# A two-block transformer kernel on one core: batches 1 to 3 of the first projection move into the first attention, and stacks are loaded in chunks of 512 tokens

## The reference, cut to what matters

```python
# block 0 attention, per batch and head
scores = alpha * tanh(q @ k.T / beta)
scores = scores + lam * (tanh(x @ hex_w.T) @ tanh(x @ hex_w.T).T / 2)
scores = scores + 2 * sig * (hexc @ Mh[h] @ hexc.T) / 6        # hexc = tanh(x @ q6_w.T)
out = softmax(causal(scores)) @ v
# block 1 attention
q, k = rope(x @ Wq.T), rope(x @ Wk.T)
out = softmax(causal(q @ k.T / 4)) @ v
```

## Time and profile before

| stage | us from the span's start | length, us |
|---|---|---|
| setup | 0 to 33.8 | 33.8 |
| projection 0, first to last matmul | 39.9 to 289.5 | 249.6 |
| from there to the first score matmul | 289.5 to 342.85 | 53.4 |
| attention 0 | 342.85 to 2521.3 | 2178 |
| rest of block 0, projection 1 | 2521.3 to 3040.7 | 519 |
| loads before attention 1 | 3040.7 to 3069.5 | 29 |
| attention 1 | 3069.5 to 4235.5 | 1166 |
| rest of block 1 | 4235.5 to 4547.3 | 312 |

### The profile page before, as it was taken

One profiled execution on the slowest core, in us unless ns is written; L12 is line 12 of the kernel. 1 busy time (PEld: TensorE's weight loads), 2 busy tenths in 40 slices (PEclk: granted clock), 3 DMA queues, 4 the chain that ended last, 5 costly groups with the idle time before them and its releaser, 6 DMA issues. The chain is left out here.

```text
span 4547.3 us, 67109 instructions
## 1 busy us (share of the span) xinstructions
PE 3916.2 (86%) x23290; PEld 1495.0 (33%) x23298; DVE 2646.7 (58%) x4835; ACT 3480.4 (77%) x3199; POOL 454.1 (10%) x407
## 2 busy tenths in 40 slices
PE   6958888888888888888888767649999999999787
PEld 3422222222222222222222554323333233333466
DVE  5537777777777777777777787851111110111488
ACT  2429999999999999999999213329999999999433
POOL 3530000000000000000000125640000000000133
PEclk9979999999999999999999988879999999999999
DMA  5872222012222112222202445652122221212232
GB/s 166 253 220 52 55 56 55 22 37 56 55 56 55 34 25 56 56 55 55 49 17 48 139 129 161 195 170 78 47 82 61 67 81 47 84 48 82 90 97 83
DMA packets 270543, 372.13 MB, mean 82 GB/s; under 512 B 27499, under 2 KB 214667, under 8 KB 265529
## 3 DMA queue, kind: packets, MB, share of 16 engines
q1 hardware_dynamic: 270244, 368.27, 29.6%
HBM read 238.14 MB, written 130.02 MB: 81 GB/s over the span
## 5 line engine op out<-in xcount | busy, mean ns | idle before, releaser
L861 DVE SCALAR_TENSOR_TENSOR att_prob<-att_tanh,alpha,ps 128x512 f32<-128x512 f32 (+3 forms) x2584 | 1583.5, 661 | 523.7 <-ACT att_tanh L795 352.1
L722 PE MATMUL ps<-att_q,att_k 96*128 96x512 bf16 (+7 forms) x5172 | 1233.3, 352 | 189.9 <-DMA att_v<-v_ones 101.7
L749 PE MATMUL ps<-att_prob,att_v 128*32 128x512 f32 (+3 forms) x10304 | 1213.0, 543 | 11.0 <-ACT att_prob L807 6.2
L795 ACT ACTIVATE att_tanh<-ps,rbeta 128x2048 f32<-128x2048 f32 (+3 forms) x646 | 1111.4, 1720 | 122.7 <-PE ps L722 122.7
L802 ACT ACTIVATE att_prob<-ps 128x1024 f32<-128x1024 f32 (+3 forms) x1290 | 1068.2, 906 | 124.6 <-PE ps L724 114.2
L807 ACT ACTIVATE att_prob<-att_prob 128x2048 f32<-128x2048 f32 (+3 forms) x645 | 1072.0, 1662 | 51.0 <-DVE att_prob L861 48.7
L733 PE MATMUL ps<-att_f,att_g 75*128 75x512 bf16 (+3 forms) x2584 | 855.0, 358 | 182.8 <-DVE att_prob L861 157.1
L722 PEld LDWEIGHTS ps<-att_q,att_k 96*128 96x128 bf16 (+1 forms) x5172 | 424.1, 98 | 1053.4 <-ACT att_prob L802 430.8
L831 DVE STREAM_TRANSPOSE att_ot<-ps 128x512 f32<-128x512 f32 x128 | 91.3, 713 | 1047.4 <-PE ps L749 1010.1
L733 PEld LDWEIGHTS ps<-att_f,att_g 75*128 75x128 bf16 x2584 | 236.6, 97 | 1066.7 <-DVE att_prob L861 1037.8
L749 PEld LDWEIGHTS ps<-att_prob,att_v 128*32 128x32 f32 x10304 | 203.1, 108 | 370.7 <-issue 142.5
(11 more groups left out here) (132 smaller groups left out, 2620.1 us busy)
## 6 DMA issues: line engine op xcount, KB each, us to landing
att_v<-v_ones SPq DMA_DIRECT2D x34, 1024.0 KB
v_ones<-proj_vs SPq DMA_DIRECT2D x128, 256.0 KB, 3.5
att_q<-q_parts SPq DMA_DIRECT2D x102, 256.0 KB
att_k<-k_parts SPq DMA_DIRECT2D x102, 256.0 KB
att_q<-q_parts SPq DMA_DIRECT2D x204, 128.0 KB
att_k<-k_parts SPq DMA_DIRECT2D x204, 128.0 KB
q_parts<-proj_parts SPq DMA_DIRECT2D x64, 384.0 KB, 3.4
k_parts<-proj_parts SPq DMA_DIRECT2D x64, 384.0 KB, 3.0
```

Source lines behind the costliest of these rows:

```text
L722: mm = pe.matmul(out, st[u]["k"][:, h, kb * P:(kb + 1) * P], st[u]["q"][:, h, g * TG + off:(g + 1) * TG], start=True, stop=not mask)
L749: mm = pe.matmul(ps[VW * h:VW * (h + 1), O0 + g % 2, off:TG], st[u]["v"][:, kb, h * VW:(h + 1) * VW], prob[:, k % R, h, off:TG], start=kb ...
L795: th.done(act.activation(tanh_s[:, k % 2, :, off:TG], ps[:, QK0:QK0 + HQ, off:TG], ACT.Tanh, scale=kn["rbeta"][:, 0:1]))
L861: sc.done(dve.scalar_tensor_tensor(prob[:, k % R, h, off:TG], tanh_s[:, k % 2, h, off:TG], kn["alpha"][:, 0:1], ps[:, E0 + h % 2, off:TG], ...
```

## The change

1. `project_phase` of layer 0 handles batch 0 only (`NB=1`). It reads x already transposed (`x0_t`, prepared on the host), so the transposes on TensorE and their copies on ScalarE are gone for layer 0.
2. Batches 1 to 3 of that projection are 108 units inside attention 0: 12 groups of 512 tokens with nine units each (g, q, q, k, k, f, f, v, v). A unit starts at the end of steps 2, 6, 10, ... of each batch, 36 in its 160 steps. TensorE does the unit's matmuls into bank 7, ScalarE takes tanh of g, VectorE copies the others out (in the next step, between heads 1 and 2), GpSimd splits q, k, f and g by itself, and SyncE stores them.
3. Bank 7 is taken from the output: in layer 0 the output has one bank (`OU = 1`), and the first weigh of a query group waits for the transpose of the group before.
4. Parts of `normalise` are taken ahead of head 0 instead of between heads 1 and 2.
5. Stacks are loaded by chunk of 512 tokens into rings (3 of q and f, 6 of k, g and v), 26 DMAs a chunk in layer 0 and 14 in layer 1. The rows in DRAM are ordered so that each partition reads one run. g is stored once instead of once per quad; projection 1 stores each q and k tile by quad, in four DMAs.
6. In layer 1 the mask matmuls are gone. VectorE takes the minimum with a table (`keep`) after exp, two instructions per diagonal step, and weigh(k) waits for it. weigh lags by two steps instead of one.
7. The steps past the last set are gone in both layers.

```diff
-    LAG = 2 if layer == 0 else 1
+    LAG = 2
+    QU, KU = 3, 6
+    QK0, E0, O0, BG = 0, 4, 6, 7
+    OU = 1 if layer == 0 else 2
+    EVERY = 4
+    def unit_at(S):
+        b, s = divmod(S, NHQ * NST)
+        u, rest = divmod(s - 2, EVERY)
+        return b * (GB * NU) + u if b < B - 1 and rest == 0 and 0 <= u < GB * NU and N_UNIT else None
...
+            def project(j):
+                X, kind, m, tile, n = unit(j)
...
+                bg_ev.wait(pe, j - 1)
+                if kind == "f":
+                    mm = pe.matmul(ps[0:n, BG], kn["Cq"][:].rearrange("p q e h -> p (q e h)")[:, m * n:(m + 1) * n], f12[:, X % 2], start=True, stop=True)
+                elif kind == "v":
+                    for t in range(2):
+                        at_t = slice((2 * m + t) * P, (2 * m + t + 1) * P)
+                        for c in range(DC):
+                            mm = pe.matmul(ps[:, BG, t * D:(t + 1) * D], xt_s[:, X % 2, c, at_t], wv_s[:, c, :], start=c == 0, stop=c == DC - 1)
+                else:
+                    for c in range(DC):
+                        lhs = w12_s[:, c, :] if kind == "g" else (wq_s if kind == "q" else wk_s)[:, c, m * P:(m + 1) * P]
+                        mm = pe.matmul(ps[0:n, BG], lhs, xt_s[:, X % 2, c], start=c == 0, stop=c == DC - 1)
+                bg_ps.done(mm)
...
             def weigh(S):
...
+                elif diag:
+                    kept.wait(pe, (it * ND + kb) * 2 + 1)
...
                 if kb == 0:
-                    o_tr.wait(pe, set_of(i, k) * GB + g - 2)
+                    o_tr.wait(pe, n - OU)
...
+            for S in range(N + LAG):
...
+                if layer == 0 and S < N:
+                    extra(S, 2)
+                    extra(S, 3)
+                if unit_at(S) is not None:
+                    project(unit_at(S))
...
+            def evict(j):
+                X, kind, m, tile, n = unit(j)
+                if kind == "v":
+                    bg_ps.wait(dve, j)
+                    v_out.wait(dve, m, X - 1)
+                    bg_ev.done(dve.tensor_copy(vs[:, m, :, :, 0:HD], ps[:, BG].rearrange("p (t h d) -> p t h d", t=2, h=H)))
+                elif kind != "g":
+                    bg_ps.wait(dve, j)
+                    low.wait(dve, tile - 2)
+                    bg_ev.done(dve.tensor_copy(raw[0:n, tile % 2], ps[0:n, BG]))
...
+            def diagonal(S):
+                it, g, kb, off, *_ = at(S)
+                for pair in range(2):
+                    pr.wait(dve, S * 2 + pair)
+                    block = prob[:, S % R, 2 * pair:2 * pair + 2, off:off + P]
+                    kept.done(dve.tensor_tensor(block, block, kn["keep"][:].unsqueeze(1).to_broadcast([P, 2, P]), ALU.min))
...
                 for h in range(HQ):
-                    if h == 2:
-                        normalise(i, due, 2 if g <= 1 else 1)
+                    if h == 0:
+                        normalise(due, 2 if g <= 1 else 1)
+                    if h == 2 and S > 0 and unit_at(S - 1) is not None:
+                        evict(unit_at(S - 1))
...
+            for n in range(QU):
+                load(n)
+                if layer == 0 and n == 0:
+                    for name, t in (("wq", wq_s), ("wk", wk_s), ("wv", wv_s), ("w12", w12_s)):
+                        sp.dma_start(t[:], w[name]).then_inc(w_in, 16)
+                    load_x(0)
+                    load_x(1)
+            LATE = LAG + 3
+            for S in range(LATE, N + LATE):
+                it, g, *_, last = at(S - LATE)
+                n = it * GB + g
+                if last:
+                    if n + QU < NG:
+                        o_tr.wait(sp, n)
...
+                        load(n + QU)
+                    store_o(n)
+                if unit_at(S - LATE) is not None:
+                    store_unit(unit_at(S - LATE))
```

More of the change, by code:

```diff
@@ L42 @@
 MASKED = -1.0e30
+KEEP = 3.0e38
 BOUND = 60.0
@@ new lines, in weigh @@
+            def weigh(S):
+                it, g, kb, off, diag, last = at(S)
+                n, c = it * GB + g, it * GB + kb // CB
+                if layer == 0:
+                    pr.wait(pe, S)
+                elif diag:
+                    kept.wait(pe, (it * ND + kb) * 2 + 1)
+                else:
+                    pr.wait(pe, S * 2 + 1)
+                if kb == 0:
+                    o_tr.wait(pe, n - OU)
+                for h in range(HQ):
+                    mm = pe.matmul(ps[VW * h:VW * (h + 1), O0 + n % OU, off:TG], v_s[:, c % KU, kb % CB, h * VW:(h + 1) * VW], prob[:, S % R, h, off:TG], start=kb == 0, stop=last)
+                pv.done(mm)
@@ L809, in _, with feature @@
-            for k in range(W):
-                step(0, k)
-            for i in range(B * NHQ // U):
-                for k in range(W, NB + W):
-                    step(i, k)
+            def feature(j):
+                X, kind, m, tile, n = unit(j)
+                if kind == "g":
+                    bg_ps.wait(act, j)
+                    if X >= 2:
+                        low.wait(act, tile - 2 * NTL)
+                    bg_ev.done(act.activation(f12[:, X % 2], ps[0:NF, BG], ACT.Tanh))
@@ L866, in _ @@
-            for i in range(B * NHQ // U):
-                due = []
-                for k in range(W, NB + W):
-                    step(i, k, due)
-                assert not due
-def row_max_phase(nc, kn, layer):
+            due = []
+            for S in range(N + LAG + 1):
+                if S > LAG and at(S - LAG - 1)[-1]:
+                    due += [(S - LAG - 1, part) for part in range(4)]
+                if S < N and layer == 0:
+                    sums(S, due)
+                else:
+                    if S < N and at(S)[4]:
+                        diagonal(S)
+                    normalise(due, len(due))
@@ new lines, in _ @@
+            assert not due
+        if layer == 0:
+            @block.gpsimd
+            def _(pool):
+                for c in (hi, rest, mid, low):
+                    c.start(pool)
+                for j in range(N_UNIT):
+                    X, kind, m, tile, n = unit(j)
+                    if kind == "v":
+                        continue
+                    u = tile % 2
+                    src = f12[:, X % 2] if kind == "g" else raw[0:n, u]
+                    bg_ev.wait(pool, j)
+                    parts_out.wait(pool, u, tile // 2 - 1)
+                    hi.done(pool.tensor_copy(parts[0:n, u, 0], src))
+                    hi.wait(pool, tile)
+                    low.wait(pool, tile - 1)
+                    rest.done(pool.tensor_tensor(rem[0:n], src, parts[0:n, u, 0], ALU.subtract))
+                    rest.wait(pool, tile)
+                    mid.done(pool.tensor_copy(parts[0:n, u, 1], rem[0:n]))
+                    mid.wait(pool, tile)
+                    low.done(pool.tensor_tensor(parts[0:n, u, 2], rem[0:n], parts[0:n, u, 1], ALU.subtract))
```

554 lines of the change are left out of this document (325 added, 229 removed).

## The result

The kernel after takes 4608.8 us (median of 4, 4602.7 to 4614.3), the kernel before 4552.4 in the same runs: ratio 1.0122, 95% interval 1.0100 to 1.0144. It is slower by 1.2%. The forecast was 4460, with a range of 4370 to 4575.

What follows compares the result with a forecast made beforehand. TensorE was taken to bound projection 0 and attention 1, ScalarE attention 0. From 4549.15 us, -194 + 187 - 2 - 11 - 11 - 58 - 2 + 1.5 = -89.5 gave 4460 us, range 4370 to 4575.

Steps and rivals of the forecast that it cites:

- (b): Attention 0, third step of a query group: weigh waits for transpose; 0.8 us without unit, 2.5 with q, k, v, 1.55 f.
- Projection 0 and the start: Start to first score matmul: 205.8 us less, mostly from projection 0 handling one batch without transposes (-194).
- The wait for chunk 1: Start of attention 0: chunk 1 lands at 43.8, group 0 is over at 33.5, so 10 us of wait.
- (a): Attention 0, unit in the middle of full steps: exp late by 1.15 us for q, k, v, 0.6 g, 0.25 f.
- (c): Attention 0, unit in step r2 (steps 10, 22, 38), slack only 0.1: 1.6 us more, f 0.7.
- (d): Attention 0, step 2, r2 and third step at once: 2.4 us with a unit, 0.3 without.
- Between the attentions: From attention 0's last output transpose to attention 1's first matmul: 25 us less.
- Attention 1: First matmul to last output transpose: 54 us less; masks off TensorE save 58 over 64 groups, bounds 20 and 80.
- The slower rival: Attention 0: unit and boundary delays add up in full, 353 us in place of 187, total 4626 us; chance 0.15 or 0.13.
- its mark: Sign deciding for the slower rival: idle time of ScalarE in attention 0 over 390 us, from 118.
- Units hide: Rival: TensorE's 280 free us in attention 0 take the units, only the boundaries' 43 remain; 4316 us; chance 0.08.

Runs made afterwards that it cites:

- Run 3: The kernel after, units and one output bank kept, with the transpose of a finished output issued one step earlier in attention 0; 4418.8 us, ratio 0.971.
- run 2: The kernel after without units (first projection does all four batches ahead of attention 0), still with one output bank; 4572.6 us, ratio 1.004.
- Run 5: The kernel after plus seven unread matmuls in front of the weigh that waits for the transpose; 4511.2 us, ratio 0.992 to the kernel before.
- run 9: As run 10, with each piece of a unit issued ahead of its step's third extra matmul, where TensorE waits; 4288.5 us, ratio 0.943.
- run 7: The kernel after with q, k and g units cut into four pieces and the transpose one step earlier; 4386.0 us, ratio 0.964.
- run 10: As run 7, with VectorE's transpose and its copy of a unit moved ahead of the step's first sum; 4338.9 us, ratio 0.954.
- run 8: As Run 3, with whole units two steps later; meant for a group's last step, but none landed there; 4452.1 us, ratio 0.978.

## Why the prediction was wrong

**The step that failed** is (b), the boundary with one output bank, priced at 0.8 us without a unit and 2.5 with one. It let TensorE be idle 1.8 us, then work on at full clock, and put the clock at nothing in the sum. The idle time was right (1.65 at 651.90); the clock behind it was not, and the price of the wait at full clock was too low as well. Attention 0 took 2485 us, over the 2440 that the forecast had named as a sign that it is wrong. Against the 133.1 us of a set with nothing of this, a set with units has 25.3 more. A line through its 11 sets has 0.30 us for each us of half clock; with 23.9 us of it in the mean that is 7.2 for the clock. Run 3 shows 13.2 for the units without the boundary's wait, 1.6 of them for its own 5.5 us of half clock, so 11.6. The other 6.5 are the waits (4.6 in run 2, without units). The forecast had, in the mean over slots filled and empty, 12.0 for the units, 2.7 for the waits and 0 for the clock; in the sets without units it had 2.7, and 8.0 was measured, 4.4 of them clock (16.2 us of half clock at run 2's 0.27) and 3.6 waits. So a set with units cost 10.6 us more than forecast: 7.2 for the clock, 3.8 for the waits, less 0.4 for the units. Over 12 and 4 sets that is 148 us; the shorter undisturbed set (133.1 for 134.8) gives 27 back, and 121 are left, against the 120 to be explained. The split rests on fitted lines and is rough. Run 5 is the kernel after with most of its clock back: 4511 us, inside the forecast's own range of 4400 to 4530.

Point by point:

- **Projection 0 and the start:** -202.3 for -205.8. Its last matmul ends at 101.3 us (98 forecast), its bound is TensorE, right. The wait for chunk 1 was 4 us of TensorE's and 5.4 of ScalarE's, not 10, as the first group's matmuls ran at the lower level of the clock (four scores 1.87 us, for 1.04 in the earlier trace rows) and took up more of the time:

```profile
140.55 1.87 PE L819 MATMUL ps<-att_q,att_k 96*128 96x512 bf16 x4 [39.23 <-DMA att_v<-v_ones]
160.86 1.89 PE L819 MATMUL ps<-att_q,att_k 96*128 96x512 bf16 x4 [4.04 <-DMA att_v<-v_ones]
```

- **(a), (c), (d), the units:** right in sum, 12.0 a set forecast and 11.6 from run 3. The single prices were not measured one by one. VectorE's copy takes 682 ns (0.65 taken), and the sums 743 ns beside GpSimd, as 0.68 between starts had it:

```profile
L923 DVE COPY att_raw<-ps x72: 678/682/686, 185.7 to 1966.0; 128x512 f32<-128x512 f32 x48, 96x512 f32<-96x512 f32 x24
```
```profile
L968 DVE SCALAR_TENSOR_TENSOR att_prob<-att_tanh,alpha,ps 128x512 f32<-128x512 f32 x1792 | 1237.8, 743 | 532.8 <-PE ps L828 320.4 <-ACT att_tanh L889 201.3 <-PE ps L830 5.5
```

- **Between the attentions:** -21.5 for -25, right.
- **Attention 1:** the direction right, the size not: a set fell by 2.6 us and not 3.6, since 64 masks at 0.06 less 0.24 of waits were taken. A mask is worth 0.04 us here. ScalarE still waits for TensorE 51.3 us in 1070, from 80.6 in 1100; what holds the rest was not tested.

```profile
ACT att_prob L895 <- PE ps L819: 51.3, 153, 0.5
```

- **The slower rival** came within 18 us of the time, and its mark was met: ScalarE was idle 417 us in attention 0 (2485.3 less 2068.7), over 390. That its total was so near is luck. It had 19.8 us a set for the units, and run 3 has 13.2; it had no price for the clock, which took 7.2. Its price of the boundaries, 7.2 a set, was nearer than mine: 6.5 with units and 3.6 to 4.6 without, for my 2.7. What I missed was in the profile: the earlier trace rows show TensorE with 0.6 us of slack at full clock, and at half clock the 2.65 us of matmuls in a step would be 5.3 against ScalarE's 3.65. The profile before already had 59 us at the lower level; I read its 0.99 as a fixed number and not as something that the change could move.
- **Units hide** was wrong for this order of instructions, but nearly right for another: in run 9 they cost 2 us a set. That its 4288.5 lies under the 4316 of this rival is also due to boundaries that no longer cost anything and to the shorter undisturbed set.

## What to carry to other kernels

Where TensorE has little slack, an added wait has two prices: its length, and what the work behind it costs at half clock. Price both, and read the granted clock of the stretch before anything else when a result is worse than the sum. To tell them apart, put unread matmuls into the wait: if the kernel gets faster with more work, the clock had a part in it. Work that is to fill gaps is best cut small and issued where the engine waits: with the single bank, units and boundaries together cost 25 us a set here with whole units behind a wait, 13 with the transpose ahead of that wait (run 3), 9 with units in four pieces as well (run 7), 6 with VectorE's copies ahead of its sums (run 10), and 2 with the pieces where TensorE waits (run 9). And look in the trace whether an edit put the work where you meant it: run 8 did not.

## What the hardware did that I had not expected

Seven matmuls that nobody reads made a kernel 98 us faster (4608.8 to 4511.2), though TensorE then has 6 us more to do per set. A wait of 1.65 us, in which the clock fell to 0.50, was followed by 8.8 us at that level in which TensorE had no gap at all: there, being busy again did not give the clock back at once. And removing 90 us of waits, 1.6 us each in the mean, gained 190 us (run 3).
